# The key term of a graph attention layer: from a product on TensorE to a sum in the mask on GpSimd

## The reference

```python
# first layer
h = relu(fa[:, :, None, :] + fb[:, None, :, :])
att = softmax(einsum('bijo,o->bij', h, W2) + where(adj > 0, 0.0, NEG_INF))
# second layer
vu = edge_attr @ U2
iv = edge_attr @ W2
lr = leaky_relu(vu[:, :, None, :] + iv[:, None, :, :], 0.2)
scores = einsum('bijc,c->bij', lr, yita[:, 0])
scores = where(edge_adj > 0, scores, -1e12)
alpha = softmax(scores, axis=2)
agg = leaky_relu(einsum('bij,bjc->bic', alpha, edge_attr), 0.2)
emb = leaky_relu((agg + (1.0 + beta) * edge_attr) @ linW.T + linb, 0.2)
```

## Time and profile before

| | us |
|---|---|
| median of 3 runs | 6147.97 (6147.73 to 6156.0) |
| the profiled execution | 6155.54 |
| its span, first to last instruction | 6153.4 |
| PE busy | 5958.3 |
| DVE busy | 5287.3 |
| ACT busy | 5271.3 |
| POOL busy | 717.9 |
| L207, matmuls of the hidden groups | 3563.5 |
| L329, hidden units on DVE | 3481.1 |
| L253, hidden units on ACT | 3435.5 |
| L119, masks of the additive layers | 181.1 |

### The profile page before, as it was taken

How to read it: one execution, slowest core, us unless ns; L and a number is a source line. 1 busy time by engine, 2 the same in 40 slices (tenths; PEclk the granted TensorE clock), 3 DMA queues, 4 the chain that set the end, 5 groups by cost and what they waited for, 6 DMA issues and landing times. The chain is left out here.

```text
span 6153.4 us, 131415 instructions
## 1 busy us (share of the span) xinstructions
PE 5958.3 (97%) x53428; PEld 2697.5 (44%) x53428; DVE 5287.3 (86%) x9011; ACT 5271.3 (86%) x6073; POOL 717.9 (12%) x505
## 2 busy tenths in 40 slices
PE   8999999999999999999999999966699999999999
PEld 2333333333333333333333333333366667666766
DVE  7999999999999999999999999956477777777777
ACT  7999999999999898998989989946388888888888
POOL 0000000000000000000000000035212212211221
PEclk9999999999999999999999999977699999999999
DMA  1000000000000000000000000024100000000000
GB/s 40 18 18 19 18 18 18 18 18 18 19 18 19 18 19 18 18 18 15 18 18 18 18 15 18 12 79 120 38 23 23 20 23 23 23 20 23 23 23 10
DMA packets 108733, 147.60 MB, mean 24 GB/s; under 512 B 15785, under 2 KB 83369, under 8 KB 108140
## 3 DMA queue, kind: packets, MB, share of 16 engines
q1 hardware_dynamic: 108140, 139.19, 7.4%
HBM read 137.07 MB, written 2.10 MB: 23 GB/s over the span
## 5 line engine op out<-in xcount | busy, mean ns | idle before, releaser
L253 ACT ACTIVATE a_hidden<-a_B,a_A 128x1024 f32<-128x1024 f32 x3200 | 3435.5, 1139 | 288.5 <-PE apsS L207 284.7
L329 DVE TENSOR_SCALAR a_hidden<-a_B,a_A 128x1024 f32<-128x1024 f32 x4992 | 3481.1, 766 | 200.5 <-PE apsS L207 175.0
L207 PE MATMUL apsS<-a_hidden,a_w_sel 128*32 128x512 f32 x32768 | 3563.5, 594 | 2.8 <-DVE a_hidden L329 2.8
L207 PEld LDWEIGHTS apsS<-a_hidden,a_w_sel 128*32 128x32 f32 x32768 | 1045.8, 110 | 2407.4 <-issue 2023.9
L692 ACT ACTIVATE Z<-m3S,edge 128x1024 f32<-128x1024 f32 x512 | 570.0, 1113 | 367.7 <-PE m3S L631 367.7
L742 DVE CUSTOM_DVE_ANT_0 Z<-Z,mask 128x1024 f32<-128x1024 f32 x512 | 624.6, 1220 | 165.5 <-ACT Z L692 164.5
L700 ACT ACTIVATE Z<-Z,negm 128x1024 f32<-128x1024 f32 x512 | 589.2, 1151 | 1.1 <-DVE negm L748 0.6
L119 POOL TENSOR_SCALAR a_mask<-a_adj_in 128x1024 f32<-128x1024 int32 x128 | 181.1, 1415 | 3440.6 <-DVE small L338 2951.8
L643 PEld LDWEIGHTS m3T<-ident,Z 128*128 128x128 f32 x4096 | 453.5, 141 | 261.0 <-issue 261.0
L643 PE MATMUL m3T<-ident,Z 128*128 128x128 f32 x4096 | 549.5, 276 | 7.6 <-DVE PT L755 5.3
L755 DVE COPY PT<-m3T 128x512 f32<-128x512 f32 x512 | 354.0, 691 | 217.6 <-PE m3T L643 213.2
(11 more groups left out here) (151 smaller groups left out, 2961.2 us busy)
## 6 DMA issues: line engine op xcount, KB each, us to landing
a_adj_in<-adj SPq DMA_DIRECT2D x128, 512.0 KB, 3.6
adj_in<-adj SPq DMA_DIRECT2D x128, 512.0 KB, 4.2
out<-yn SPq DMA_DIRECT2D x64, 32.0 KB, 1.5
wvT<-L_wvT SPq DMA_DIRECT2D x1, 130.0 KB
wq<-L_gnn_Wq SPq DMA_DIRECT2D x1, 128.0 KB
wk<-L_gnn_Wk SPq DMA_DIRECT2D x1, 128.0 KB
wp<-L_gnn_Wp SPq DMA_DIRECT2D x1, 128.0 KB
a_w_sel<-L_gnn_W SPq DMA_DIRECT2D x2, 0.2 KB, 6.8
```

Source lines behind the costliest of these rows:

```text
L207: last = pe.matmul(psS[k % 2][32 * q:32 * q + 32, h * HALF:(h + 1) * HALF], w["sel"][layer][:, 30 - 2 * p:62 - 2 * p], hidden[:, (k * GROU ...
L253: act.activation(hidden[:, (k * GROUPS + p) % SLOTS, q, :], B2[:, g % 2, :], ACT.Relu, bias=A2[:, g % 2, pair:pair + 1]).then_inc(hid_act, 1)
L329: dve.tensor_scalar(hidden[:, (k * GROUPS + p) % SLOTS, q, :], B2[:, g % 2, :], A2[:, g % 2, pair:pair + 1], 0.0, ALU.add, ALU.max).then_i ...
```

## The change

The key term is computed directly on all 128 partitions: the column of weights `u` is repeated 128 times, so that one product of `u` (64x128) with half of the key projections (64x512) gives the key term of 512 keys on every partition (`key_rows`, two per batch). ACT copies it into a new buffer `TB` (128 x 2 x 1024, f32). POOL adds the row of the tile's batch to each mask of layer 2 with a second operation, `tensor_tensor`, behind a new semaphore `mask_made`; `mask_ready` now follows that sum. POOL waits for `key_rows` at the first tile of a batch, and ACT waits for the masks of batch g - 2 before it overwrites `TB`. The BF16 split on DVE, the turning on PE, `T3`, the ones and the product with them go. Layer 2's first hidden group starts the accumulation, as layer 1's does. The side jobs are placed anew: `key_rows` behind group 12 of tile 4 and behind group 4 of tile 5.

```diff
     def projection(g):
         jobs = [("turn_x", g, 0), ("turn_x", g, 1), ("keys", g, 0), ("keys", g, 1), ("queries", g, 0)]
-        return jobs + ([("key_term", g, 0), ("turn_t", g, 0), ("turn_t", g, 1)] if g >= nb else [])
+        return jobs + ([("key_rows", g, 0), ("key_rows", g, 1)] if g >= nb else [])
...
-    AHEAD = {(0, 0): 0, (0, 1): 1, (1, 0): 2, (1, 1): 3, (2, 1): 4, (4, 1): 5, (6, 0): 6, (6, 1): 7}
+    AHEAD = {(0, 0): 0, (0, 1): 1, (1, 0): 2, (1, 1): 3, (2, 1): 4, (4, 1): 5, (5, 0): 6}
...
                 gp.nop(nofuse=True)
+                m, row = k - nb * tiles, k // tiles % 2
+                if m < 0:
+                    gp.tensor_scalar(mask[:, k % 2, :], adj_in[:, k % 2, :], NEG, -NEG, ALU.mult,
+                                     ALU.add).then_inc(mask_ready, 1)
+                    return
                 gp.tensor_scalar(mask[:, k % 2, :], adj_in[:, k % 2, :], NEG, -NEG, ALU.mult,
-                                 ALU.add).then_inc(mask_ready, 1)
+                                 ALU.add).then_inc(mask_made, 1)
+                if m % tiles == 0:
+                    gp.wait_ge(aux_out, done("key_rows", k // tiles, 1))
+                gp.wait_ge(mask_made, m + 1)
+                gp.tensor_tensor(mask[:, k % 2, :], mask[:, k % 2, :], TB[:, row, :], ALU.add).then_inc(mask_ready, 1)
...
-                elif what == "key_term":
-                    for t in range(tiles):
-                        last = pe.matmul(psA[:, t:t + 1], B2[0:C, g % 2, t * P:(t + 1) * P], w["u"], start=True, stop=True)
-                elif what == "turn_t":
-                    pe.wait_ge(t_split, g - nb + 1)
-                    pe.nop(nofuse=True)
-                    for t in range(4):
-                        last = pe.transpose(psA[0:3, t * P:(t + 1) * P], tsplit[:, 4 * i + t, :], ident)
+                elif what == "key_rows":
+                    last = pe.matmul(psA[:, :], w["u"], B2[0:C, g % 2, i * HALF:(i + 1) * HALF], start=True, stop=True)
...
-                                         start=p == 0 and layer == 0, stop=p == GROUPS - 1)
+                                         start=p == 0, stop=p == GROUPS - 1)
...
-            def add_key_term(k):
-                g, j = divmod(k, tiles)
-                if j == 0:
-                    pe.wait_ge(aux_out, done("turn_t", g, 1))
-                pe.wait_ge(min_ready, k - 1)
-                for h in range(n // HALF):
-                    pe.matmul(psS[k % 2][:, h * HALF:(h + 1) * HALF], w["ones"], T3[:, g % 2, h * HALF:(h + 1) * HALF],
-                              start=True, stop=False)
...
-                        if nb * tiles <= k + 1 < K:
-                            add_key_term(k + 1)
...
-                elif what == "key_term":
-                    if g > nb:
-                        act.wait_ge(t_split, g - nb)
-                    act.activation(tcol, psA[:, 0:tiles], ACT.Copy).then_inc(aux_out, 1)
-                elif what == "turn_t":
-                    act.activation(T3[:, g % 2, half], psA[0:3, :], ACT.Copy).then_inc(aux_out, 1)
+                elif what == "key_rows":
+                    if g >= nb + 2:
+                        act.wait_ge(mask_ready, (g - 1) * tiles)
+                    act.activation(TB[:, g % 2, half], psA[:, :], ACT.Copy).then_inc(aux_out, 1)
...
-            def split_key_term(i):
...
-                    if p == 7 and j == 5 and nb <= g + 1 < G:
-                        split_key_term(g + 1 - nb)
...
-            dve.tensor_scalar(w["u"], ycol, -GAT_SLOPE, None, ALU.mult)
+            dve.tensor_scalar(w["u"], ycol.to_broadcast([C, P]), -GAT_SLOPE, None, ALU.mult)
```

More of the change, by code:

```diff
@@ L51, in additive_layers @@
     adj_in, mask, Z, PT, OT, y = buf["adj_in"], buf["mask"], buf["Z"], buf["PT"], buf["OT"], buf["y"]
-    tcol, thigh, tsplit, T3 = buf["tcol"], buf["thigh"], buf["tsplit"], buf["T3"]
+    TB = buf["TB"]
     stats, mv, vare, rstd, den, rden = (buf[s] for s in ("stats", "mv", "vare", "rstd", "den", "rden"))
@@ L96, in additive_layers @@
         weighed, o_out = sem("weighed"), sem("o_out")
-        aux_made, aux_out, t_high, t_rest, t_split = sem("aux_made"), sem("aux_out"), sem("t_high"), sem("t_rest"), sem("t_split")
+        aux_made, aux_out, mask_made = sem("aux_made"), sem("aux_out"), sem("mask_made")
         inverted, leaky, u_ready, lin_leaky = sem("inverted"), sem("leaky"), sem("u_ready"), sem("lin_leaky")
@@ L452, in _ @@
             dve.tensor_scalar(w["sel"][1], w["sel"][1], GAT_SLOPE - 1.0, None, ALU.mult)
-            dve.tensor_scalar(w["u"], ycol, -GAT_SLOPE, None, ALU.mult)
+            dve.tensor_scalar(w["u"], ycol.to_broadcast([C, P]), -GAT_SLOPE, None, ALU.mult)
             dve.tensor_scalar(w["beta1"], w["beta1"], 1.0, None, ALU.add)
             dve.tensor_tensor(w["fold"], w["ident"][:, 0:C], w["ident"][:, C:P], ALU.add)
-            dve.memset(w["ones"], 1.0)
 HEADS = 8
@@ L869, in build @@
                        mask=sg("a_mask", [P, 2, n]), Z=sg("a_Z", [P, n])[:, :], PT=sg("a_PT", [P, n]),
-                       OT=sg("a_OT", [P, tiles, P])[:, :, :], y=sg("a_y", [P, tiles * C])[:, :], tcol=sg("a_tcol", [P, tiles])[:, :],
-                       thigh=sg("a_thigh", [P, 2, tiles], BF16), tsplit=sg("a_tsplit", [P, tiles, 3]),
-                       T3=sg("a_T3", [3, 2, n], BF16), stats=sg("a_stats", [P, tiles, 6]), mv=sg("a_mv", [P, tiles, 2]),
+                       OT=sg("a_OT", [P, tiles, P])[:, :, :], y=sg("a_y", [P, tiles * C])[:, :], TB=sg("a_TB", [P, 2, n]),
+                       stats=sg("a_stats", [P, tiles, 6]), mv=sg("a_mv", [P, tiles, 2]),
                        vare=sg("a_vare", [P, tiles])[:, :], rstd=sg("a_rstd", [P, tiles])[:, :],
@@ L876, in build @@
             w_a, w_b = [sg(f"a_w_a{i}", [C, 2, P]) for i in range(2)], [sg(f"a_w_b{i}", [C, P]) for i in range(2)]
-            u, lin_w, lin_b, beta = sg("a_u", [C, 1]), sg("a_lin_w", [C, C]), sg("a_lin_b", [P, C]), sg("a_beta", [P, 1])
-            ycol, fold, ones = sg("a_ycol", [C, 1]), sg("a_fold", [P, C]), sg("a_ones", [3, P], BF16)
+            u, lin_w, lin_b, beta = sg("a_u", [C, P]), sg("a_lin_w", [C, C]), sg("a_lin_b", [P, C]), sg("a_beta", [P, 1])
+            ycol, fold = sg("a_ycol", [C, 1]), sg("a_fold", [P, C])
             xv = a["x"].rearrange("(t p) c -> p t c", p=P)
@@ L891, in build @@
             w = dict(a=w_a, b=[t[:, :] for t in w_b], sel=[t[:, :] for t in w_sel], u=u[:, :], lin=lin_w[:, :],
-                     lin_b=lin_b[:, :], beta1=beta[:, :], fold=fold[:, :], ones=ones[:, :], ident=ident[:, :])
+                     lin_b=lin_b[:, :], beta1=beta[:, :], fold=fold[:, :], ident=ident[:, :])
             additive_constants(nc, w, ycol[:, :])
```

## The result

The changed kernel takes 6123.8 us, the median of five runs (6123.14 to 6124.27), against 6151.19 us (6147.73 to 6156.0) of the kernel before beside it: a ratio of 0.9954, 95% interval 0.994 to 0.9969. That is 27 us faster, where 33 us and a time of 6115 us (6147.97, the median of the first three runs, less 33) had been forecast. A later set of five runs gave the same ratio of 0.9954 (0.994 to 0.9968). The profiled execution of the changed kernel has a span of 6122.3 us.

A forecast was written before the change was run, and what follows sets the result against it. PE was taken to bound the additive layers; its work falls 46.5 us, less 13.1 us of DVE excess, a gain of 33 us. From 6155.54 that gives 6122.5, less 7.6 carried over: 6115 us, range 6097 to 6165.

The forecast's parts named there:

- PE's side: PE in the additive layers: without the key term's old steps its sum is 46.5 us shorter, a layer 2 batch 249.6 us.
- The step on S: Time POOL's sum takes from DVE per layer 2 tile: taken as 2.0 us, between 0.79 and 3.4.
- DVE against PE: Layer 2 batches: DVE needs 250.5 us against PE's 249.6 and becomes the bound; 13.1 us of the gain is lost.
- the formula: DVE's work per layer 2 batch: 234.5 us plus eight times the sum's toll, compared with PE's 249.6.
- the head start: DVE's lead in layer 2: 1.2 us of its total excess of 14.3 us is absorbed, once.
- Where PE waits: Layer 2 tiles: DVE's excess appears as a wait of PE before `turn`, on ACT's exponential.
- the slip of 5.4 us: Between the masked minimum and PE's `turn`: about 2.7 + 2.7 us by which DVE may fall back free.
- The 7.6 us carried over: Whole time: the median shown, 6147.97, lay 7.6 us below the profiled execution less 33's starting point; subtracted again, giving 6115.
- PE stays the bound: Rival in layer 2: toll under 1.88 us, so the whole 46.5 us is gained, 6101 us; chance 0.20.
- The slow case: Rival in layer 2: POOL's sum holds DVE 3.4 us, DVE is the bound outright, 6203 us; chance 0.16.
- The clock: Rival on PE: waits before `turn` bring more clock falls, 6140 us; if three falls go, 5 us gained; chance 0.04.
- How long POOL holds DVE: Shared port: DVE's 2-port operations are blocked for the whole POOL instruction; half a documented 4497 ns add is 2.25 us.

The follow-up runs named there:

- the run of the sum alone: The kernel before, with each mask of layer 2 also getting a POOL sum with zeros and the key term staying on PE: 6158.73 us, one run.
- The comparison: The kernel before, with its masks made by a comparison and a product instead of a product and a sum: 6154.87 us, one run.
- the two sums: The changed kernel with a second POOL sum, with zeros, behind the first: 6252.99 us.
- the power of 128x8: The changed kernel with POOL's sum replaced by a power of 128x8 numbers, the key term left out of the scores: 6106.28 us.

## Why the prediction was right

**PE's side.** The new batch had been computed as 249.6 us; without the sum it is 249.75. The ones product at 0.53 us per tile and the 1.06 us of `key_rows` hold: L165 starts at 2394.82 and the next group at 2395.88 in the changed kernel. Over the additive layers PE's side is 3956.0 - 3905.8 = 50.2 us shorter. In that are the three falls of the clock, 5.1 us, which I had only as a side of a rival; without them it is 45.1 against the 46.5 forecast. The falls go when the ones product alone is taken out, so `linear` by itself isn't the reason, as the rival of that run had it. Why `turn`, L219 and `linear` together bring the clock down in three batches and not in the others stays open; in the run of the sum alone there were three as well, but one of them in another batch.

**The step on S** was a choice between 0.79 and 3.4 us, and 2.0 was 0.13 too low: close, but by a guess within a wide range. By the prediction's own 6.3 us for 0.1 us this should have cost 8 us of the gain. It didn't, because of the next step.

**DVE against PE.** At S = 2.13 the formula gives 234.5 + 17.0 = 251.5 us per batch; measured, 251.35. The last seven tiles are 8.5 us longer than without the sum, about as computed (7.7 at S = 2.0, 8.6 at 2.13). What was too small is the head start: 1.2 us were to be absorbed once. In fact batch 8 shows no wait at all and batch 9 waits of 0.4 us, where the formula has an excess of 2.3 and 1.8 us: 3.7 us were absorbed. The four full batches behind them lose 1.58 us each, where the formula has 1.9. In all the waits lengthen the stage by 16.5 us, where 13.1 were forecast and 21 would have followed with the right S. Two errors of 5 to 8 us cancelled, and the falls of the clock gave 5.1 more: the stage's gain of 33.7 us agrees with the 33 forecast partly by luck.

**Where PE waits.** I had all of the excess ahead of `turn`. A tile shows 0.36 us there, and 0.63 us one group later, where DVE's unit held up by the sum is due. What was wrong here is the slip of 5.4 us: once DVE has no lead, its stall behind the minimum hits the next hidden group, not only the exponential. It changed nothing in the total, which is DVE's length.

**The 7.6 us carried over** from the profiled execution to the median had no source in the trace, and it didn't hold. The changed kernel's profiled execution took 6124.1 us, 0.3 off its median, and the profile of before lay above its own later median of 6151.19 by 4.4. So 6115 was 9 us too low. Of the 7.6 us the table shows where such differences arise: layers 3 and 4, whose code is the same, took from 2112.9 to 2121.2 us.

**The rivals.** PE stays the bound: false by 0.25 us of toll per tile; without the sum it is what happens, at 6105 where 6101 was computed. The slow case, S of 3.4 us from L573: the sum didn't reach it, and the row was a poor measure of a toll. The comparison shows that an operation of L573's form, 4.18 us beside busy DVE, stops DVE for 1.6 us only. Where the changed kernel would be slower than before was also off: with 33 us of gain at S = 2.0 and 6.3 us for each 0.1, break-even is at S = 2.5, not 2.7; 2.7 is where the loss would be clear of the scatter. The clock: no fall is left in the additive layers although PE now waits in most batches.

**How long POOL holds DVE.** The mechanism came from the Trainium skill (SBUF - State Buffer, on the shared port pair): an exclusive lock, which the first to start has for its whole instruction. Half the length of the 2048-wide sum in the Trainium skill (GPSIMD Engine Reference, section 3.1) had put S between 2.0 and 2.25, an estimate; the trace's 2.13 agrees. For the two sums and the plain mask the toll follows the instruction's length, less 0.5 to 0.6 us (2.13 of 2.70, 1.03 of 1.6, 0.79 of 1.42). Two runs disagree with "the whole instruction": the power of 128x8 runs 2.42 us beside DVE at no toll, and the compared mask stops it twice for 0.78 us in 4.18. So the length alone doesn't give the toll; how much data is moved, and when within the instruction, matters too, and which of the two decides was not separated.

## What to carry to other kernels

POOL's idle time isn't free for data of DVE's size: count, beside every full-size POOL operation, how much longer the DVE operations get (here 0.79 us for the mask with its one input of 128x1024, 2.13 for the sum with two), and compare it with what DVE would need for the same work (1.22). Then hold the new total of each engine per period against that of the bound: a toll costs nothing up to the slack (1.03 us cost nothing here, where the slack was put at 1.88 per tile) and nearly all of what lies beyond it (a second 2.13 was paid in full). When a change makes the bound engine faster, the next one's slack is the first thing to work out again, and moving one unit of work between the two others may give back all that was lost.

## What the runs showed of the hardware

A sum of 128x1024 f32 on POOL takes 2.70 us beside busy DVE and takes 2.13 us from it; the same on 512 columns takes 1.03 us, so for this operation the toll goes with the elements. A POOL power of 128x8 f32 takes 2.42 us and nothing from DVE. A compare-and-multiply of 128x1024 takes 4.18 us and stops DVE twice, 0.78 us each, with DVE at full rate between. DVE itself does the sum of 128x1024 f32 in 1.22 us. The same code of layers 3 and 4 took between 2112.9 and 2121.2 us in different profiles, as much as the times of the kernel before scatter (6147.73 to 6156.0).
